# A two-layer graph network on one core: where VectorE empties the accumulation banks of the count matmuls, and how soon TensorE reuses them

## The reference, cut to what matters

```python
h = jnp.maximum(_layernorm(x), 0.0)
msg = sum over r of (h[src] * (edge_type == r)) @ weight[r]
x = x + segment_sum(msg, dst)
h = jnp.maximum(_layernorm(x), 0.0)
agg, cnt = segment_sum(h[src], dst), segment_sum(1, dst)
out = (agg / max(cnt, 1)) @ W_l + b_l + h @ W_r
out = out + zeros.at[dst].set(edge_attr @ W_e + b_e)
x = x + out
```

## Time and profile before

| what | value |
|---|---|
| median of 3 runs | 4618.67 us (4602.07, 4618.67, 4619.43) |
| profiled execution, its own time | 4602.55 us |
| its span | 4600.7 us |
| granted TensorE clock over the span | 0.822 |
| PE, DVE, ACT, POOL busy | 65%, 76%, 46%, 67% |
| first gather of slot 0; product of slot 624 ends | 321 us; 4384 us |

### The profile page before, as it was taken

One profiled execution on the slowest core, in us unless ns is written; L12 is line 12 of the kernel. 1 busy time (PEld: TensorE's weight loads), 2 busy tenths in 40 slices (PEclk: granted clock), 3 DMA queues, 4 the chain that ended last, 5 costly groups with the idle time before them and its releaser, 6 DMA issues.

```text
span 4600.7 us, 83711 instructions
## 1 busy us (share of the span) xinstructions
PE 3003.2 (65%) x23324; PEld 2426.3 (53%) x23325; DVE 3500.4 (76%) x17508; ACT 2121.8 (46%) x7155; POOL 3103.8 (67%) x3190
## 2 busy tenths in 40 slices
PE   1464555555565666565676677766777777777799
PEld 1123444444444544454565555655666666666689
DVE  5564778778788877887888888887888888888833
ACT  0243455545455554554545455454554554545400
POOL 1017777777777777777777777777777777777700
PEclk9985767767777777787787788878988989989999
DMA  9872333333323433242342433423423333332379
GB/s 101 262 307 61 116 92 116 114 110 110 101 85 109 136 120 113 92 131 76 100 142 87 126 117 91 124 74 112 121 82 111 113 94 107 109 89 76 111 286 383
DMA packets 315349, 575.64 MB, mean 125 GB/s; under 512 B 124155, under 2 KB 227259, under 8 KB 303515
## 3 DMA queue, kind: packets, MB, share of 16 engines
q1 hardware_dynamic: 135494, 443.69, 26.9%
q0 software_dynamic: 101568, 105.81, 11.4%
q10 hardware_dynamic: 77842, 20.86, 3.6%
HBM read 334.10 MB, written 248.81 MB: 127 GB/s over the span
## 4 chain that ended last, share of the span: by engine, by line
POOL 59%; issue 20%; PE 9%; DMA 6%; ACT 2%; DVE 2%; ACTq 1%; another core or an unknown queue 1%; POOLq 0%; SPq 0%; DVEq 0%
POOL msg L475 58%; DMA msg<-rel_table,istage 5%; PE ps L1143 4%; PE ps L1043 2%; PE ps L485 2%; ACT arena L884 2%; POOL wrel L714 1%; ACTq L846 1%; DVE onehot L1247 1%; DMA arena<-counts 1%; PE ps L1127 1%; DMA arena<-in_dst 0%; PE ps L1069 0%; DVE arena L670 0%
## 5 line engine op out<-in xcount | busy, mean ns | idle before, releaser
L475 POOL DMA_INDIRECT msg<-rel_table,istage x3125 | 3040.3, 973 | 953.7 <-issue 939.9
L884 ACT CAST arena<-ps 128x392 bf16<-128x392 f32 x3136 | 1326.5, 511 | 1945.7 <-PE ps L1069 1930.8
L485 PE MATMUL ps<-onehot,msg 128*81 128x128 f32 x6250 | 1083.5, 336 | 1124.7 <-DMA msg<-rel_table,istage 1082.3
L485 PEld LDWEIGHTS ps<-onehot,msg 128*81 128x81 f32 x6250 | 925.3, 192 | 1225.2 <-DMA msg<-rel_table,istage 1099.7
L1387 DVE TENSOR_SCALAR batch<-iota_h,wrel 128x196 bf16<-128x196 bf16 x4312 | 1248.2, 294 | 0.0
L1386 DVE TENSOR_SCALAR batch<-iota_h,wrel 128x128 bf16<-128x128 bf16 x4312 | 1173.5, 275 | 0.0
L503 DVE TENSOR_SCALAR onehot<-iota_w,arena 128x128 f32<-128x128 f32 x3125 | 684.9, 299 | 544.0 <-PE ps L485 542.6
L1069 PE MATMUL ps<-batch 128*128 128x196 bf16 x4312 | 761.6, 287 | 186.6 <-DVE batch L1387 88.9
L893 ACT ACTIVATE msg<-attr,arena 128x16 f32<-128x16 f32 x3125 | 693.6, 317 | 4.5 <-DMA attr<-in_edge_attr 4.4
L1127 PE MATMUL ps<-arena 128*128 128x192 bf16 x7238 | 690.0, 254 | 0.0
L1127 PEld LDWEIGHTS ps<-arena 128*128 128x128 bf16 x7238 | 636.6, 102 | 7.4 <-issue 0.3
(11 more groups left out here) (149 smaller groups left out, 1210.9 us busy)
## 6 DMA issues: line engine op xcount, KB each, us to landing
arena<-counts SPq DMA_DIRECT2D x458, 224.0 KB, 4.3
rel_table<-arena SPq DMA_DIRECT2D x98, 512.0 KB, 3.5
msg<-rel_table,istage POOLq DMA_INDIRECT x3125
counts<-arena SPq DMA_DIRECT2D x10, 3136.0 KB
arena<-counts SPq DMA_DIRECT2D x28, 896.0 KB, 11.9
attr<-in_edge_attr SPq DMA_DIRECT2D x125, 200.0 KB
counts<-arena SPq DMA_DIRECT2D x8, 2688.0 KB
arena<-counts SPq DMA_DIRECT2D x31, 672.0 KB, 10.8
```

What stands on the lines that cost most here:

```text
L475: pool.indirect_dma_start(msg[:, k, 0:D], None, table, bass.IndirectOffsetOnAxis(ap=istage[:, k:k + 1].bitcast(U32), axis=0)).then_inc(got ...
L485: mm = pe.matmul(ps[0:rows, bank, 0:WIN], msg[:, k, 0:rows], onehot[:, k, :], start=(k == 0), stop=(k == K - 1))
L884: nc.scalar.copy(cblk[:, h, :, u * WU * WD:(u + 1) * WU * WD].rearrange("p t (w d) -> p w t d", d=WD), unit_cols(b, u).rearrange("p w (t d ...
```

## The change

Two edits. In the planner a mult may begin one slot after the mult two before it ended, and not two. In VectorE's order the results stand first in a slot and not last. The rest of the code is unchanged.

```diff
@@ planner
             if not mults or mults[-1]["at"] == mults[-1]["t1"]:
-                if len(mults) >= 2 and mults[-2]["end"] + 2 > c:
+                if len(mults) >= 2 and mults[-2]["end"] + 1 > c:
                     break
@@ block.vector
                 for c in range(LAST):
+                    for k, m in enumerate(mults):
+                        if c == m["end"] + 1:
+                            mult_result(k)
                     if c % NG == 1 and NG < c <= SLOTS + 1:
                         add_superblock(c // NG - 1)
                     mid_slot(c)
...
                             if u == UB - 1 and b % 2 == 1 and b + 1 < NT:
                                 take_keys((b + 1) // 2)
-                    for k, m in enumerate(mults):
-                        if c == m["end"] + 1:
-                            mult_result(k)
```

## The result

The changed kernel takes 4695.93 us (median of 4 runs, 4694.31 to 4703.22) where the kernel before takes 4613.12 (4 runs, 4602.07 to 4619.43). The ratio is 1.018, interval 1.0156 to 1.0205. The profiled execution took 4695.2 us. The sign was forecast, the size was not: 83 us between the medians where the sum said 31, and 4696 us lies just inside the upper end of the range (4700).

The account below looks back on a forecast made before the run. GpSimd's gathers were taken to pace the stage, VectorE having little to spare. Gather stage +54 us (35 + 6 + 5 + 8) and tail -23 gave +31: 4634 on the profiled time, 4650 on the median, so 4642 us, range 4597 to 4700.

Parts of the forecast that it names:

- where I said 23: Tail after the last product: 273 matmuls move out of it, so it gets 23 us shorter.
- VectorE must wait, by the order of the instructions: VectorE's slot: results wait for a mult queued behind units whose one-hots VectorE writes last; 2.4 us at the place read.
- the fourth case of the prediction: Gather stage: gathers hide all the added wait and the tail's -23 stands, 4580 to 4596 us; chance 0.12.
- 1184 matmuls x 90 ns = 107 us: Slots 500 to 624: VectorE's wait for the count matmuls ahead of results, 107 us at 90 ns each.
- 40 + 107 = 147: Slots 500 to 624: VectorE's added waits, 73 hand-overs of 0.55 us (40 us) plus 107 us of matmuls.
- 138.8 to spare: Slots 375 to 499: VectorE's existing waits of 138.8 us can absorb added waits; 122.5 us in the last 125 slots.
- the place from which I read the 90 ns: Kernel before, 2421.98 to 2423.88 us: 21 count matmuls on TensorE, taken as 90 ns each.
- the second case: Stage loses more than 100 us, with 105 ns a matmul and full attribute-load holds: +108, net +85; chance 0.11.
- The sum had 54 us: Gather stage: total loss of 54 us, from 35 + 6 + 5 + 8.
- 35 + 5 + 8: Last block: 35 waits beyond VectorE's spare, 5 late gathers before result slots, 8 lateness carried from the middle block.
- 6 for the loads: Attribute loads behind room loads in the SP queue hold ScalarE; three more in the last block, +6 us.
- Slots 0 to 374 covered, the middle block even: Slots 0 to 374: 160 us of waits covered; slots 375 to 499: 115 against 138.8, attribute loads using the rest.

Follow-up runs that it names:

- the order alone: Changed kernel with the planner's number put back to 2, results still first in VectorE's slot: 4793.11 us, ratio 1.0376 to the kernel before.
- a later place: Changed kernel with results moved later in VectorE's slot: after the one-hots of slot c+3, 4582.55 us; after the third unit, 4582.49 us.
- the planner's edit without the other: Kernel before with only banks reused one slot sooner, VectorE's results still last in its slot: 4588.55 us, ratio 0.9936.
- the repeats: Changed kernel with TensorE making each unit's matmuls three times into the same place, except a slot's last unit: 4659.72 us, ratio 1.0086.
- repeats and loads: Changed kernel with repeated unit matmuls and attribute loads on ScalarE's queue, also called both repairs: 4644.82 us, ratio 1.0063.
- when taken away alone: Changed kernel with attribute loads of superblocks 1 to 124 issued by ScalarE on its own queue, not by SP: 4679.41 us, ratio 1.0156.
- the kernel that waits for nothing: Changed kernel with the results after the third unit of VectorE's slot: 4582.49 us, ratio 0.9923 to the kernel before.

## Why the prediction had the sign and not the size

**What bounds the kernel, and the tail.** Right. The stage was GpSimd's pace, VectorE was the next, and the tail lost 23.8 us where I said 23.

**VectorE must wait, by the order of the instructions.** Right, and shown from both sides: the order alone makes the wait (753 us of it), a later place takes it away. Also right: the case that the denser plan alone hides in the gathers. It is the planner's edit without the other, and the fourth case of the prediction in another kernel: 4589 us.

**The price of the wait.** This is the step that failed: "21 x 90 ns" a slot and "1184 matmuls x 90 ns = 107 us", with nothing in the sum for a lower clock. In the changed kernel a count matmul took 112 ns, and 110 in the last 125 slots. There VectorE's waits came to 161.5 us where the sum had 40 + 107 = 147, and in slots 375 to 499 to 145.4 where it had 113, more than the 138.8 to spare. (The mean wait of 2.4 us, where I had said some 1.7, misleads: it takes in 97 waits of 3.3 us in slots 0 to 374, many of which stand in place of waits for products of late gathers: those of L503 fell from 542.6 to 171.3 us.) With the repeats that hold the clock up and the attribute loads out of the way the last block has 146.2 us, which is the 147 of the sum, and the middle one 126.2, less than it can spare.

What the order does to TensorE is seen in its own waits: it waited for one-hots 1488 times, 690 us in all, where before it was 344 times and 136 us. The matmuls of the units come in small pieces, since VectorE works just ahead of them, and the mult that VectorE waits for then often runs at the lower clock, at 156 ns a matmul; the slower mult makes VectorE later still. Of the large groups that had four or more stops of TensorE, of 0.15 us or longer, in the 5 us ahead of them (a stretch that I chose for the count), 68 of 159 ran at the lower level; of the others 1 of 124. The second profile of the changed kernel has 65 of 157 and 5 of 126. In the kernel before, only 7 groups had so many stops ahead of them. But this feeding does not always bring the clock down: the place from which I read the 90 ns had it too, with waits of 0.34 to 0.54 us ahead of its mult, and ran at 1.00:

```profile
2415.90:2421.80 5.90, 3.88 (x33) 2.73 (x34) 5.90 (x33) 3.48 (x9) 4.60 (x5) 1.00 0.49 142
2421.90:2423.90 2.00, 2.00 (x25) 2.00 (x25) 2.00 (x12) 1.72 (x9) 1.58 (x2) 1.00 0.17 40
```

One place at the upper level could not give the price of 1184 matmuls. I had named them as the largest unknown and put 105 ns into the second case, at 0.11; and I had said that the granted clock of the last block would stay near 0.9. It did (0.89). A mean over 810 us does not tell at which matmuls the clock is low.

By the Trainium skill, TensorE: Matmul & The Clock Gate, section A second HAM failure mode: psum-queue depth-cycling, a TensorE that idles briefly and often between groups of matmuls swings between the two clocks. The trace agrees, with 69 groups at 0.6 or less against 3 before. I had taken only the two prices from that page and not asked which would hold; and the formula from which I had them is there (section Back-to-back issue gap) that of a matmul by itself, of which the section says that it counts too little where small matmuls each load their weights.

**The account.** GpSimd's idle time before its gathers, counted in the trace by blocks of slots, shows where the loss lies and what each repair takes of it:

| slots | before | changed (two profiles) | with the repeats | repeats and loads |
|---|---|---|---|---|
| 0 to 374 | 572.7 | 583.2, 584.2 | 575.1 | 572.8 |
| 375 to 499 | 190.5 | 210.1, 205.6 | 196.4 | 190.5 |
| 500 to 624 | 190.5 | 240.4, 250.4 | 231.2 | 222.9 |
| all | 953.7 | 1033.7, 1040.2 | 1002.8 | 986.1 |

The sum had 54 us, all in the last block: 48 of plain wait (35 + 5 + 8), 6 for the loads and 0 for the clock. Measured are 80 and 87 us. The clock is 31 of the 80 (8, 14 and 9 us in the three blocks), the loads 17 (14 when taken away alone) and the plain wait 32. So the sum without the clock came near, 54 against 49, though partly by luck: the loads were too cheap in it (4.5 us of ScalarE in each of the 12 places, which were counted rightly) and the plain wait too dear. What it left out was the clock.

In time the same steps are larger: from 4696 us the repeats take 36 us, the loads some 9 to 15 more, and between 4645 us and the kernel that waits for nothing are 62. The price of the place is 113 us by time and 80 to 87 by GpSimd's idle time. The other 26 to 33 are no wait of GpSimd. In the two profiles of the changed kernel the gathers themselves took 13 to 15 us longer than in the one with the results after the third unit, and the first gather began 4 to 16 us later. Between two profiles of one kernel the gathers have differed by 29 us and that start by 12, so this part stays open.

The net of +83 us is the second case of the prediction (+85, at 0.11). Its 105 ns were near and its middle block (+20) was right, but its last block was too dear (+78, where 50 to 60 were measured), so that the match of the net is partly luck. One slip changes nothing: 39 more room loads are 273 tiles of 32 KB, 8.9 MB and not 8.6.

**Slots 0 to 374 covered, the middle block even.** Wrong in the changed kernel: idle time grew by 10 to 12 us up to slot 374 and by 15 to 20 in slots 375 to 499. I had written that the prediction is wrong if the stage stretches already before slot 375, and it did, a little. It is right in the kernel with both repairs (572.8 and 190.5 us). So it was the clock and the loads that used up the cover. Single waits of VectorE for L1127, up to 11.1 us, do not explain it: with both repairs in they are still up to 14.1 us.

**The place of the reduction.** What the prediction did not see is how little was needed. One step later, after the one-hots, 275 us of waits cost nothing, since in both late blocks they are less than VectorE has to spare (77.5 of 138.8 and 93.1 of 122.5 us).

What is not settled: how the 32 us of plain wait in the last block divide between the hand-over, the matmuls and the lateness carried over, what makes the clock fall after some of the stretches with many short waits and not after others, and the 26 to 33 us above.

## What to carry to other kernels

An instruction that waits for the engine which works through the queue behind it belongs at least one hand-over and one work item after the last thing it fed that engine; count what must happen between the two and put that much other work ahead of the wait. Here the 1.0 us of one-hots was already enough, since what waits remained fitted into what the waiting engine could spare. A resource can be reused sooner without its release being moved first: here the planner's number alone was worth 26 us, and the release had only to come before the next user, not at once. When the price of a wait is taken from a row, ask whether the waiting engine's lateness would change the pace of the other one, above all TensorE's clock, and look at many such rows and not one.

## What the runs showed of the hardware

Repeating matmuls made a kernel faster: 10,000 more of them, 36 us less, with the granted clock over the execution at 0.932 and not 0.825. In the changed kernel TensorE's clock fell at 4054.05 us while matmuls had run in every microsecond since 4049.7, in pieces of 0.3 us with waits of 0.4 to 0.5 us between them; in the kernel before it stayed up through like pieces, with one product and 11 count matmuls among them, from 2415.9 to 2421.8. In the kernel before, where TensorE waited 1082 us for gathers and 496 us in the changed one, it was up at 283 of 286 large groups. Single gathers of GpSimd, 0.945 us in the median, took 11.2 and 12.5 us in one profile of the changed kernel and 9.6 us in one of the kernel before, at different places; the sum of all gathers differs by up to 30 us between executions, and did so between two of the same kernel (3040.3 and 3069.7 us).
